# Soft MoE inside a fused two-layer kernel: a chunk's four gate/up products in one block, and the down products moved into their own chunk

## The reference, cut to what matters

```python
x = _layernorm(x, norm_g, norm_b)
se = _layernorm(slot_embeds, slot_g, slot_b) * scale
logits = jnp.einsum('bnd,esd->bnes', x, se)
dispatch = jax.nn.softmax(logits, axis=1)
combine = jax.nn.softmax(logits.reshape(x.shape[0], x.shape[1], -1), axis=-1)
slots = jnp.einsum('bnd,bnes->besd', x, dispatch)
gate = jax.nn.gelu(jnp.einsum('besd,edf->besf', slots, Wg) + bg[None, :, None, :], approximate=False)
up = jnp.einsum('besd,edf->besf', slots, Wu) + bu[None, :, None, :]
eout = jnp.einsum('besf,efo->beso', gate * up, Wd) + bd[None, :, None, :]
return jnp.einsum('bns,bso->bno', combine, eout.reshape(eout.shape[0], -1, eout.shape[-1]))
```

## Time and profile before

| | |
|---|---|
| runs, median (lowest to highest) | 1910.64 us (1907.95 to 1914.26), 3 runs |
| the profiled execution | 1910.32 us, its span 1907.8 us |
| mean granted TensorE clock | 0.966 of full speed |
| busy over the span | PE 87%, DVE 58%, ACT 50%, POOL 11% |
| stage of the change | about 270 us to 1240 us: first gate product at 270.47 us, last combine at 1239 us |
| in that stretch | of 970 us PE busy 920.5, DVE 547.7, ACT 554.8, POOL 83.7; clock 0.99 |

### The profile page before, as it was taken

The page is one execution under the profiler, slowest core; times in us unless marked ns, Lnnn a source line. Parts: engine busy times, 40 slices in busy tenths (PEclk is TensorE's granted clock), DMA queues, the critical chain, the costliest instruction groups (busy, mean ns, idle before and its releaser), DMA issues. The chain is left out here.

```text
span 1907.8 us, 36117 instructions
## 1 busy us (share of the span) xinstructions
PE 1660.9 (87%) x13125; PEld 1359.3 (71%) x13125; DVE 1108.0 (58%) x2377; ACT 959.0 (50%) x1383; POOL 219.0 (11%) x209
## 2 busy tenths in 40 slices
PE   1777169999999999999999999959989987999999
PEld 1666147777777777777777777747777765888887
DVE  5886435565655555655556565445666657555555
ACT  1776235555555465555655555436656644222222
POOL 2122010010000100101001000013233220000000
PEclk9998569999999999999999999989999998999999
DMA  3000500000000000000000000030000002000000
GB/s 95 1 0 1 158 1 2 1 2 1 2 1 2 3 2 1 2 1 3 2 2 1 2 2 1 2 90 1 2 0 0 0 1 67 7 5 11 5 5 11
DMA packets 31170, 23.48 MB, mean 12 GB/s; under 512 B 3161, under 2 KB 28721, under 8 KB 30898
## 3 DMA queue, kind: packets, MB, share of 16 engines
q1 hardware_dynamic: 31026, 21.56, 4.1%
HBM read 19.46 MB, written 2.10 MB: 11 GB/s over the span
## 5 line engine op out<-in xcount | busy, mean ns | idle before, releaser
L664 DVE SCALAR_TENSOR_TENSOR hidden<-psU,b_cols,gelu 128x512 f32<-128x512 f32 x256 | 191.3, 749 | 269.5 <-ACT gelu L778 168.5
L778 ACT ACTIVATE gelu<-psG,b_cols 128x512 f32<-128x512 f32 x256 | 176.2, 688 | 175.8 <-PE psG L127 170.3
L863 PE MATMUL psDown<-w_down,hidden 128*64 128x128 f32 x4096 | 252.3, 276 | 1.1 <-DVE expert_out L670 0.8
L863 PEld LDWEIGHTS psDown<-w_down,hidden 128*64 128x64 f32 x4096 | 221.3, 137 | 33.1 <-issue 23.7
L1517 ACT ACTIVATE silu<-psG 128x512 f32<-128x512 f32 x128 | 76.5, 598 | 212.8 <-PE psG L127 208.0
L624 POOL TENSOR_TENSOR dispatchT<-dispatchT,dispatch_inv 128x512 f32<-128x512 f32 x64 | 66.9, 1045 | 828.6 <-DVE dispatch_inv L750 828.6
L125 PE MATMUL psG<-slots_hi,w_gate_hi 128*128 128x512 f32 x256 | 117.6, 459 | 26.5 <-DVE slots_lo L720 14.5
L720 DVE TENSOR_TENSOR slots_lo<-psM,slots_hi 128x512 fp32r<-128x512 f32 x128 | 82.5, 686 | 87.3 <-ACT slots_hi L808 87.3
L1579 PEld LDWEIGHTS psY<-w_downT,hidden 128*128 128x128 f32 x1024 | 123.9, 191 | 5.8
L1579 PE MATMUL psY<-w_downT,hidden 128*128 128x128 f32 x1024 | 124.3, 275 | 0.0
L1471 DVE TENSOR_TENSOR hidden<-psU,silu 128x512 f32<-128x512 f32 x128 | 88.5, 692 | 54.6 <-PE psU L127 50.2
(11 more groups left out here) (312 smaller groups left out, 3545.1 us busy)
## 6 DMA issues: line engine op xcount, KB each, us to landing
ctx<-in_ctx SPq DMA_DIRECT2D x8, 512.0 KB, 7.1
x<-in_x SPq DMA_DIRECT2D x4, 512.0 KB, 6.0
combine<-in_L_ffn_Wg SPq DMA_DIRECT2D x1, 2048.0 KB
combine<-in_L_ffn_Wu SPq DMA_DIRECT2D x1, 2048.0 KB, 17.6
out<-x SPq DMA_DIRECT2D x8, 256.0 KB, 2.3
w_kv<-in_L_xattn_Wkv SPq DMA_DIRECT2D x1, 1024.0 KB
w_down_raw<-in_L_ffn_w_down SPq DMA_DIRECT2D x1, 1024.0 KB, 10.0
hidden<-in_L_ffn_slot_embeds SPq DMA_DIRECT2D x1, 512.0 KB
```

What stands on the lines that cost most here:

```text
L664: dve.scalar_tensor_tensor(hid[e][:, half, :], U[half][:], bcol[:, 1, 4 * ch + 2 * e + half:][:, 0:1], gel[half][:], ALU.add, ALU.mult).th ...
L778: act.activation(gel[half][:], G[half][:], ACT.Gelu, bias=bcol[:, 0, 4 * ch + 2 * e + half:][:, 0:1]).then_inc(s["gelu"], 1)
L863: last = pe.matmul(DN[e * SEQ:(e + 1) * SEQ, j, :], hid[e][:, half, b * SEQ:(b + 1) * SEQ], wd[:, 2 * ch + e, half, :], start=(half == 0 a ...
```

## The change

PE, ACT and DVE get a new order; no operation is added or removed, and the waits inside the helpers stay. PE now issues the four gate_up in one run at the chunk's start, then lb, combine of the chunk before (g 1), td, down of this chunk (g 0), ct_t, down of this chunk (g 1), sl, combine of this chunk (g 0), then tx or la. ACT does the four gelus in a row; DVE does `expert_out` of the chunk before (g 1), the four `hidden`, the two lb steps, `expert_out` (g 0), `finish`, `slots_lo`. After the last chunk only one combine is left. The diff, cut where lines only move:

```diff
@@ vector: body
                     if has_core(o):
-                        hidden(k, 0, ch, 0)
                         if exists(o, ch, -1):
                             expert_out(k - 1, 1, (ch - 1) % CH)
-                    if exists(o, ch, 2):
...
-                    if has_core(o):
+                        hidden(k, 0, ch, 0)
                         hidden(k, 0, ch, 1)
-                        if ch == 0 and not (isinstance(o, int) and o == 0):
-                            finish(o - 1, 1 - par)
...
                     if has_core(o):
                         hidden(k, 1, ch, 0)
                         hidden(k, 1, ch, 1)
+                    if exists(o, ch, 2):
...
+                        dve.tensor_reduce(nm[:], scores, AX.X, ALU.max, negate=True).then_inc(s["lb_max"], 1)
...
+                        dve.tensor_tensor(e[:], scores, over(nm[:], SEQ, 2), ALU.add).then_inc(s["lb_shifted"], 1)
+                    if has_core(o):
+                        expert_out(k, 0, ch)
+                        if ch == 0 and not (isinstance(o, int) and o == 0):
+                            finish(o - 1, 1 - par)
                     if exists(o, ch, 1):
...
-                    if has_core(o):
-                        expert_out(k, 0, ch)
@@ scalar: body
                     if has_core(o):
-                        gelu(k, 0, ch, 0)
-                        gelu(k, 0, ch, 1)
+                        for e in range(2):
+                            for half in range(2):
+                                gelu(k, e, ch, half)
...
-                        gelu(k, 1, ch, 0)
...
-                        gelu(k, 1, ch, 1)
@@ tensor: body
                     if has_core(o):
-                        gate_up(k, 0, ch, 0)
-                        if exists(o, ch, -1):
-                            down(k - 1, 1, (ch - 1) % CH)
-                            combine(k - 1, 0, (ch - 1) % CH, o)
+                        for e in range(2):
+                            for half in range(2):
+                                gate_up(k, e, ch, half)
                     if exists(o, ch, 2):
...
-                    if has_core(o):
-                        gate_up(k, 0, ch, 1)
+                    if has_core(o) and exists(o, ch, -1):
+                        combine(k - 1, 1, (ch - 1) % CH)
...
                     if has_core(o):
-                        if exists(o, ch, -1):
-                            combine(k - 1, 1, (ch - 1) % CH)
-                        gate_up(k, 1, ch, 0)
+                        down(k, 0, ch)
...
                     if has_core(o):
-                        gate_up(k, 1, ch, 1)
+                        down(k, 1, ch)
...
                     if has_core(o):
-                        down(k, 0, ch)
+                        combine(k, 0, ch, o)
...
             walk(pe, body)
-            down(LAST, 1, CH - 1)
-            combine(LAST, 0, CH - 1)
             combine(LAST, 1, CH - 1)
```

More of the change, by code:

```diff
@@ L712, in body @@
                         hidden(k, 1, ch, 1)
+                    if exists(o, ch, 2):
+                        e = eb[ch % 2]
+                        need(dve, s["lb"], k + 3)
+                        scores = M0.rearrange("p (b n) -> p b n", b=OB)
+                        dve.tensor_reduce(nm[:], scores, AX.X, ALU.max, negate=True).then_inc(s["lb_max"], 1)
+                        need(dve, s["lb_max"], k + 3)
+                        need(dve, s["td"], k + 1)
+                        dve.tensor_tensor(e[:], scores, over(nm[:], SEQ, 2), ALU.add).then_inc(s["lb_shifted"], 1)
[3 more added lines that the diff above has]
+                            finish(o - 1, 1 - par)
                     if exists(o, ch, 1):
```

## The result

The changed kernel takes 2139.8 us (median of 4 runs, 2136.2 to 2143.1), against 1909.3 us (median of 4) of the kernel before in the same session: a ratio of 1.120, 95% interval 1.117 to 1.123. It is slower by 230 us. The forecast was 2091 us, in a range of 2050 to 2150; the time lies in the range, and 49 us of the 230 were not in the sum.

A forecast was written before the change was run, and what follows sets the result against it. The prediction took PE's stream to bound the kernel, stopping once per chunk after the slots. Its terms, -14 + 79 + 28 + 88 = +181 us on 1910.3 us, gave 2091 us, range 2050 to 2150.

The forecast's parts named there:

- a, the stream: PE's nine float32r products in one run, with changed costs of small f32 groups: net -0.22 us per chunk, -14 us.
- b, wait for the slots: Behind the slots combine (0.54 us) instead of down (1.79) covers the 2.75 us path: +1.25 us, 63 times, +79 us.
- c, wait for psDown: Second down overwrites the bank expert_out reads, with only ct_t between the downs: +0.44 us, 63 times, +28 us.
- d, gelu and hidden: Second expert's products wait for gelu and hidden to free their banks: 28 x 0.44 + 35 x 2.16 = +88 us.
- clock: Rival: PE's holes after the slots and after la drop the clock to 1.2 GHz: +106 us, 2197 us; chance 0.08.
- what follows decides what a small f32 group costs: In PE's stream, four turns take 0.36 us before a product, 0.53 before 64-column f32 matmuls: +0.17 for ct_t.
- no wait overlapped another: Rival: waits overlap; after la the gelu path starts earlier, 76 us go, 2015 us; chance 0.06.
- a net gain of grouping: Rival: runs of one type gain all 0.53 us per chunk, without new bank waits: 1877 us; chance 0.03.
- Its own uncertainty: Forecast's spread: stream bounds +14 or -20 us, the step before hidden -8, three new waits up to +36: 2063 to 2141.

The follow-up runs named there:

- Experiments one: Changed kernel with the chunk's second down moved back behind the slots and the first down cut in two halves around ct_t: 1999.6 us, ratio 1.046 to the kernel before.
- two: Changed kernel with the block of four gate_up cut into two pairs, lb, combine and td between them: 2078.4 us, ratio 1.088 to the kernel before.
- Five: Changed kernel with combine of the chunk before (g 1) moved from ahead of td to between first down and ct_t: 2114.6 us, ratio 1.107 to the kernel before.
- experiments three: Changed kernel with gate_up cut into two pairs and the second down moved back behind the slots: 1922.6 us, ratio 1.0062 to the kernel before.
- eight: Kernel before with four combineT buffers instead of two and combine (g 1) behind the down, except in chunk 0: 1866.4 us, ratio 0.978.
- experiment nine: Kernel before with four combineT buffers, combine (g 1) behind down except chunk 0, and DVE starting on a psM bank once ACT rounded it: 1845.6 us, ratio 0.967.

## Why the prediction was right, and what it missed

Per chunk, read from the warm chunks above against those of before, and times the number of chunks (one chunk stands for its kind, so the products are good to a few us):

| step | forecast | measured |
|---|---|---|
| a, the stream | -0.22 x 63 = -14 us | +0.22 x 63 = +14 us |
| b, wait for the slots | +1.25 x 63 = +79 | 2.20 - 0.96 = +1.24, x 63 = +78 |
| c, wait for psDown | +0.44 x 63 = +28 | 0.96 - 0.59 = +0.37, x 63 = +23 |
| d, gelu and hidden | 28 x 0.44 + 35 x 2.16 = +88 | 4.04 and 5.66 us, as forecast, but nothing in the last octet's 7 chunks: 21 x 0.44 + 35 x 2.16 = +85 |
| clock | 0 | about +30: 32 are left of the 232, and the count of products gives 34 |

- **b and d were right**, in mechanism and size, but for the last octet: there the second expert's products wait for nothing (a chunk takes 15.95 us against 14.33), since ACT's table load for gelu starts 0.54 us into the chunk (1387.32 - 1386.78) and not 1.06. Experiments one (b and c closed, d left) and two (d closed, b and c left) show that the waits stand by themselves; that they add was right too: 140 and 61 us came back singly, 217 together.
- **c was right**, a little large; its base is 0.59, not 0.53, since a group of turns costs 0.58 to 0.59 between other f32 groups. Five took it away.
- **a had the wrong sign.** The step that failed is "what follows decides what a small f32 group costs": it was applied to the turns and not to the downs. A down with combine behind it streams for 1.79 us, with turns or slots behind it for 1.90 (565.67 to 567.57). That is 0.21 for two; combine, td and ct_t add 0.05 to 0.06 each; and the first run after PE has waited for hidden pays the entry surcharge again (561.54 to 562.34 is 0.80, not 0.70): 0.10. Together 0.47, against the 0.44 between forecast and measured. This is reckoned from rows; five, where a down has combine behind it again and streams 1.79 (1390.45 to 1392.24), bears it out for the downs, and experiments three and eight show the sign with nothing waiting: 13.63 us a chunk grouped, 13.50 not.
- **The clock was put with the rivals**, at 0.08 and 106 us, and at nothing in the sum. It was neither all nor nothing: it fell behind a part of the holes and cost some 30 us. The argument against it was that PE works without a gap between the holes, and that the attention stage stays at 1.00; but the holes there are 1.3 us long, these 1.8 to 2.1. The trace of before held better evidence, in this very stage. Behind its first product PE has only two holes of more than 1 us, both at the start of an octet, 2.83 and 2.69 us, between long stretches of dense work; behind both the clock is at 0.50, as here at the first (PE's timeline, then the table by windows, in which the clock is the third number from the end):

```profile
635.16 0.79 PE L125 MATMUL psG<-slots_hi,w_gate_hi 128*128 128x512 f32 x1 [2.83 <-issue]
636.00:638.00 2.00, 2.00 (x5) 1.07 (x4) 0.00 (x0) 1.10 (x1) 0.00 (x0) 0.50 0.05 12
```

That was the pair of rows to put beside a forecast of 63 holes of 2.2 us. What decides between holes of one length is not shown: the same hole goes cold more often in five than in the changed kernel. The Trainium skill, TensorE: Matmul & The Clock Gate, section "A second HAM failure mode: psum-queue depth-cycling", had said that short idle times between groups of matmuls can make the clock go back and forth; the runs here agree with it, at 0.92 to 0.98 over 400 to 1200 us wherever one of the holes is open, and 1.00 once both are filled.

- **The other rivals** fell: no wait overlapped another, and a net gain of grouping showed nowhere; with nothing waiting it costs 0.13 us per chunk (experiment three).
- **That the time lies within the range is in part luck.** The sum missed 49 of 230 us. Its own uncertainty reached 2141, by +14 us for the stream and +36 for waits that might be longer. The waits were not longer; that room was filled by a stream 28 us slower than forecast and by a clock that had no term in the sum.

## What to carry to other kernels

A stream that reaches across engines is held together by what PE does between a result and its next use. Before grouping like operations, list for each bank the path until it is free, here 2.75 us after the slots and 5.66 us after la, and see what still stands between; the few tenths that a run of like products saves don't pay for one such path laid open, and here the small groups between took them back even where nothing waited. And read the same list for what to put there: the 0.54 us combine behind the down and an earlier start for DVE brought 3.3%.

## What the runs showed of the hardware

- Holes of 1.8 to 2.8 us in an otherwise busy PE brought the granted clock to 0.50 in some of the cases, for about three products (8 of 21 like chunks in the changed kernel); holes of 0.8 us and, in the attention stage, 1.3 us did not. Work without use in the hole kept it at 1.00 and made the kernel faster.
- A group of 64-column f32 matmuls (32 records) streams in 1.79 us with another such group behind it and in 1.90 with 128-column ones behind it.
- A run of nine float32r products of three 128x512 matmuls takes 6.40 us where nothing waits, the same nine spread over four places 6.82.
- DVE reading one psM bank while ACT reads the other cost neither anything: in experiment nine ACT's pair of copies takes 1.07 us as before, DVE's pair of `slots_lo` 1.29.
